# Experts' stage: VectorE forms a later group's variance inside the router's sequence of operations

## The reference

```python
h = layernorm(x) * (1 + ca) + sa
x = x + ga * attention(h)          # gated linear attention, 16 heads of 64
h = layernorm(x) * (1 + cb) + sb
# the experts' part: 8 experts, the best 2 count
p = softmax(max(h @ gate_W + gate_b, 1e-4))
comb = where(top2(p), max(p, 0.1) / sum over the two, 0)
y = einsum("bsd,edf->bsef", h, expert_W) + expert_b
x = x + gb * einsum("bsef,bse->bsf", y, comb) / 2
```

## Time and profile before

| | |
|---|---|
| median of 3 runs | 3374.94 us (3367.84 to 3376.30) |
| profiled execution | 3372.66 us |
| its span in the profile | 3370.9 us |
| mean granted TensorE clock | 0.991 of full speed |
| PE busy | 3237.4 us (96% of the span) |
| DVE busy | 2475.0 us (73%) |
| ACT busy | 1818.1 us (54%) |
| POOL busy | 1436.8 us (43%) |

### The profile page before, as it was taken

One profiled execution on the slowest core, in us unless ns is written; L12 is line 12 of the kernel. 1 busy time (PEld: TensorE's weight loads), 2 busy tenths in 40 slices (PEclk: granted clock), 3 DMA queues, 4 the chain that ended last, 5 costly groups with the idle time before them and its releaser, 6 DMA issues. The chain is left out here.

```text
span 3370.9 us, 129353 instructions
## 1 busy us (share of the span) xinstructions
PE 3237.4 (96%) x51114; PEld 2745.6 (81%) x51114; DVE 2475.0 (73%) x6681; ACT 1818.1 (54%) x4492; POOL 1436.8 (43%) x1117
## 2 busy tenths in 40 slices
PE   7999999999999999999999999999968999999999
PEld 6888888888888888888888888888856777777777
DVE  5777777776777777777777777777647878877886
ACT  5666666666666666666666666666633222222221
POOL 4444445545444444554554444455421222222222
PEclk9999999999999999999999999999988999999999
DMA  4222222222322222222223222222221111111110
GB/s 149 74 77 79 78 79 78 79 72 77 92 79 78 79 79 75 79 79 75 75 79 93 79 76 81 78 78 78 67 83 48 39 39 51 39 39 42 48 38 26
DMA packets 158613, 238.74 MB, mean 71 GB/s; under 512 B 30216, under 2 KB 82488, under 8 KB 157752
## 3 DMA queue, kind: packets, MB, share of 16 engines
q1 hardware_dynamic: 158008, 230.33, 21.6%
HBM read 194.58 MB, written 35.67 MB: 68 GB/s over the span
## 5 line engine op out<-in xcount | busy, mean ns | idle before, releaser
L447 POOL TENSOR_TENSOR qs_sb<-lam_bc,qk_sb 128x512 f32<-128x512 f32 x256 | 533.9, 2085 | 1080.7 <-DVE qk_sb L945 981.8
L554 ACT ACTIVATE kd_sb<-bank_scores,decay 128x64 f32<-128x64 f32 x2048 | 447.9, 330 | 287.7 <-PE bank_scores L820 279.0
L928 DVE SCALAR_TENSOR_TENSOR s_mid<-s_mid,lam_bc,bank_dense 128x65 f32<-128x65 f32 x1536 | 433.6, 282 | 55.1 <-DVE s_mid L928 0.3
L455 POOL TENSOR_TENSOR oT_lo<-oT,oT_hi 128x512 fp32r<-128x512 f32 x256 | 328.0, 1281 | 77.3 <-ACT oT_hi L531 77.0
L513 ACT ACTIVATE qk_sb<-bank 128x512 f32<-128x512 f32 x512 | 317.4, 620 | 50.7 <-PE bank L596 34.5
L515 ACT ACTIVATE qk_sb<-qk_sb 128x512 f32<-128x512 f32 x512 | 323.4, 632 | 16.3
L980 DVE TENSOR_TENSOR p_sb<-bank_scores,decay 128x512 f32<-128x512 f32 x256 | 176.5, 690 | 205.8 <-ACT kd_sb L554 203.8
L594 PE MATMUL bank<-wv_hi,h_hi 128*128 128x256 f32 x1024 | 307.4, 300 | 7.1 <-DVE qk_sb L943 3.3
L951 DVE TENSOR_TENSOR_SCAN decay<-a_bc,eye 128x512 f32<-128x512 f32 x256 | 311.0, 1215 | 2.0 <-DMA a_bc<-rows_dram 2.0
L1312 DVE SCALAR_TENSOR_TENSOR acc<-bank,comb,acc 128x256 f32<-128x256 f32 x512 | 230.1, 476 | 101.3 <-ACT acc L1180 91.8
L820 PE MATMUL bank_scores<-qk_sb 64*64 64x128 f32 x8192 | 287.4, 276 | 8.2 <-ACT oT_hi L531 4.3
(11 more groups left out here) (198 smaller groups left out, 8610.9 us busy)
## 6 DMA issues: line engine op xcount, KB each, us to landing
a_bc<-rows_dram SPq DMA_DIRECT2D x512, 128.0 KB, 3.0
lam_bc<-rows_dram SPq DMA_DIRECT2D x512, 128.0 KB
x_in<-in_L_attn_x_dram SPq DMA_DIRECT2D x32, 512.0 KB, 5.5
x_res<-in_L_attn_x_dram SPq DMA_DIRECT2D x32, 512.0 KB, 4.0
x_dram<-x_res SPq DMA_DIRECT2D x32, 512.0 KB, 2.9
x<-x_dram SPq DMA_DIRECT2D x32, 512.0 KB, 3.2
out_dram<-x SPq DMA_DIRECT2D x32, 512.0 KB, 2.9
ew_raw<-in_L_ffn_expert_W_dram SPq DMA_DIRECT2D x8, 256.0 KB, 5.4
```

What stands on the lines that cost most here:

```text
L447: pool.tensor_tensor(qs_sb[:, na, :], lam_bc[na][:, :], q_sb, ALU.mult).then_inc(qs_ready, 1)
L455: pool.tensor_tensor(oT_lo[:, u, :], oT32[:, :], oT_hi[:, u, :].bitcast(F32), ALU.subtract).then_inc(oT_lo_ready, 1)
L554: ins = act.activation(kd_sb[:, t, hd * DH:(hd + 1) * DH], KTR[:, hd, t * CK:(t + 1) * CK], ACT.Copy, scale=decay[:, hd, t, CK - 1:CK])
L928: dve.scalar_tensor_tensor(dst, src, lam_bc[nb][:, (ch + 1) * CK - 1:(ch + 1) * CK], U[ch], ALU.mult, ALU.add).then_inc(state_step, 1)
```

## The change

Inside groups that route the next group's tokens and have adds to do (T >= 0), the call ln_variance(T + 2) moves from behind route(T + 1) into it: between(k) issues it behind the add that follows operation 2 * NCH + 2 = 10 of twenty. NCH is 4. In group -1 it stays where it was (behind route), and in group -2 too (behind the four ln_stats). The number of instructions is the same on every engine; no DMA, no semaphore count and no other engine's order changes.

```diff
@@ -1415,17 +1415,21 @@
                             split_low(k // 2 - 1)
                     elif exists(T):
                         add(T, s, first + (k // 2 - 1 if k <= 2 * NCH else k - NCH - 1))
+                        if k == 2 * NCH + 2 and exists(T + 2):
+                            ln_variance(T + 2)
 
                 if exists(T + 1):
                     route(T + 1, (s + 1) % 2, between)
+                    if leads(T):
+                        ln_variance(T + 2)
                     adds(first + ROUTE - NCH, ADDS - BLOCK_ADDS)
                 else:
                     adds(first, ADDS - BLOCK_ADDS)
                     if exists(T + 2):
                         for ch in range(NCH):
                             ln_stats(T + 2, (s + 2) % GPB, ch)
-                if exists(T + 2):
-                    ln_variance(T + 2)
+                    if exists(T + 2):
+                        ln_variance(T + 2)
                 adds(ADDS - BLOCK_ADDS, ADDS)
                 if leads(T):
                     lo_rows = slice(2 * LO, EB_ROWS)
```

## The result

The changed kernel takes 3353.73 us (median of 6 runs, 3349.17 to 3360.70), beside 3375.62 us for the kernel before (6 runs, 3367.84 to 3377.47). The ratio is 0.994, with a 95% interval of 0.993 to 0.9949: some 20 us, or 0.6%, faster (17 to 24 by the interval). The forecast was 3351.2.

A forecast was written before the change was run, and what follows sets the result against it. TensorE, 96% busy, was taken to wait each group on the chain variance, shift, xn. 3372.66 - 23.8 + 0 = 3348.9 us, given as 3351.2 after a 2.3 us shift to the median; range 3346 to 3368.

The forecast's parts named there:

- Term 1: Experts' stage: TensorE's 29 waits for xn go, 16.8 us shown plus 0.24 us overlap each; gain 23.8 us.
- Term 2: Router on VectorE: the moved variance fills time L1368 stands held by GpSimd; cost 0, at most 0.60 us per group.
- Rival (a): Router's second half: GpSimd's power L1151 holds VectorE's L1372; TensorE waits 5.9 us in all, 3357.1 us; chance 0.25.
- Rival (b): Tenth place in the router: GpSimd's standing time doesn't cover the variance; costs 15.5 us, 3366.7 us; chance 0.14.
- (c): Router: L1368 misses the gap between L1140 and L1142, the power holds L1370; costs 35.3 us, 3386.5 us; chance 0.11.
- (d): Router: L1368 misses the gap between L1140 and L1142, the power doesn't block; costs 11.9 us, 3363.1 us; chance 0.05.
- (e): ScalarE: something else, its tile load or combT, keeps xn late, so no gain; 3375.0 us; chance 0.07.

The follow-up runs named there:

- k8: Variance behind the router's eighth operation instead of the changed kernel's tenth; 3373.82 us, ratio 1.0 to the kernel before.
- k14: Variance behind the router's fourteenth operation instead of the changed kernel's tenth, after GpSimd's large pair; 3367.77 us, ratio 0.9974 to the kernel before.
- k11: Variance behind the router's eleventh operation instead of the changed kernel's tenth, under GpSimd's second large operation; 3355.98 us, ratio 0.995 to the kernel before.
- k10_double_end: Changed kernel plus a second set of four bn_aggr into a spare tile declared last; 3358.84 us, ratio 0.9955 to the kernel before.
- k10_shift: Changed kernel plus an unused tile of 32 bytes per partition declared before var_eps, moving only addresses; 3362.11 us, ratio 0.9966 to the kernel before.
- k10_shift64: Changed kernel plus an unused tile of 64 bytes per partition declared before var_eps; 3351.21 us, ratio 0.9925 to the kernel before.

## Why the prediction was right

**What binds.** Shown: the chain from the variance to xn ended last, and with the variance early TensorE's wait went, in every version that moved it into the router, the slow k8 included.

**Term 1, 23.8 us.** Right in its size. The step from the idle time shown to what it is worth, 0.61 to 0.85 us by the earlier trace rows, was needed (the group of the earlier trace rows is the one at the turn of the loop, whose biases come late for that): the loop's groups became 0.84 us shorter (25.51 to 24.67) and the written-out ones 0.55 (25.22 to 24.67, for a wait shown as 0.32). With the shown 16.8 us alone the forecast would have been 5 us short. The reason given for the step, 0.24 us of overlap, was too simple: xn's first transposes start 0.47 us behind biases that last 0.64, an overlap of 0.17, and the other 0.06 us lie behind their start (6.55 us from the transposes to the gate matmuls before, 6.48 after). The groups gave 22.0 of 23.8. Part of the last 1.8 us lies in six groups (T = 0, 7, 12, 14, 19 and 26) in which L1252 comes 0.2 to 0.3 us late behind a late router, as it did in T = 12 before. In T = 7 and 19 VectorE stands 0.23 us before one of the router's adds, for nothing that the profile shows; the cause wasn't followed up.

**Not in the sum.** The 2.9 us by which the clock made the turn of the loop longer. They are about as much as the measured 3353.73 lies above the forecast, but single traces of one kernel differ by as much elsewhere, so this doesn't settle where the 2.5 us are.

**Term 2, 0 us.** Right, and for the reason given: k14 has the cost when the cover is missing (TensorE 0.47 us late, 0.54 expected), k11 shows that the second large operation covers as well, and k10_double_end shows the edge. One detail was wrong without harm: I had the tensor_scalar run free and L1368 asked for at once. It is held too. The time in which it is held L1368 would have been held too, so L1370 ends with L1142 as before; only the add behind L1368 starts 0.07 us later (2995.91, 7.84 us after the gate matmuls, for 7.77), which nothing waited for.

**Rival (a), the power.** Refuted: L1372 has two inputs in SBUF, was asked for 0.76 us into L1151 and took 0.18 us, and 0.17 or 0.18 in every other group. Asked for 0.18 us behind the power's start (L1373 behind L1152 in k10_double_end) or 0.26 us behind it (L1370 in k8) it isn't held either. The profile's spans on GpSimd are rough, but three places in one operation of 1.02 us leave little room for a hold. The Trainium skill's SBUF — State Buffer, section Who interferes with whom, has the second instruction block for the whole of the first. That agrees with L1140 and L1142, 1.3 us each, and doesn't with this short operation of 4 elements.

**Rival (b), no cover.** Its doubt was half right: var_eps, with one input, was held in the loop for 0.15 us. The Trainium skill's VectorE: DVE Perf Modes, section Mode 2×_2P, by which it reads through both ports, agrees with the trace here.

**Rivals (c) and (d), the missed gap.** The mechanism is real (k8, and the written-out groups of k10_double_end). The margin was read for the loop alone, as 0.19 us, and there it was wider: in k10_double_end var_eps was asked for 0.27 us later (7.76 us after the gate matmuls for 7.49), and L1368 still started 0.03 us before the second large operation, so it had been 0.3. The variance took 0.50 us up to L1368 where nothing held it, not 0.60. In the written-out groups it was narrower, 0.1 us: in the changed kernel L1368 starts 7.47 and L1142 7.58 us after the gate matmuls. By the prediction's own 0.60 us these six groups had only 0.05 to spare. That these got through is luck as much as reading. The price of (d) was too low as well: a group of k10_double_end that missed lost 0.54 us where it was written out, for 0.30, and 0.64 in the loop, for 0.42. I had counted only the router's end; the add behind L1368 also frees the bank for block 6, and k8 lost the whole gain by it where I had expected to keep half.

**(e)** didn't come about: xn started right behind combT.

## What to carry to other kernels

Look for instructions that take several times their usual length, and at what they end with. The standing time of one that is held by another engine is a free place for work that must be done early, if that work doesn't need what is held, or needs it no longer than the hold lasts. Find the edge too: here 0.3 us more put the next instruction behind a second hold in eight groups of thirty, and in most of these cost the whole gain (25.21 us a group, as before the change). And before giving an engine time back, see what its next instructions wait for; taking the holds away altogether bought nothing, because the adds behind them waited for products.

## What the runs showed of the hardware that was not expected

- A power of 4 elements per partition on GpSimd, 1.02 us long, doesn't hold a VectorE operation with two SBUF inputs (0.18 us when asked for 0.18, 0.26 or 0.76 us into it), though a 128x512 product does until it ends (L1370 in the changed kernel stands to 0.05 us behind the end of L1142).
- VectorE's float32 tensor_scalar of 4 elements per partition is held like one with two inputs (1.31 us in k8 for 0.17), bn_aggr is not (0.37 us for four beside L1140, 0.38 without it).
- 32 bytes in the start address of h and the tiles with it change the pitch of the experts' 128x512 matmuls from 0.229 to 0.233 us, 24.67 to 25.02 us per group. With 64 bytes they are 0.228 and 24.64. The granted clock was 1.00 from 2700 to 2950 us in k10_shift and in k10_shift64. Which of the moved tiles does it wasn't tried.
- A TensorE wait shown as 0.61 us costs 0.84, and one shown as 0.32 costs 0.55; 0.17 us of the difference are the overlap of the transposes with the biases before them, which a wait takes away.
- After TensorE had stood for 3.1 us, its granted clock stayed 1.00 in the kernel before and was 0.50 for the next 5.2 us in the changed one, with 0.43 us per matmul for 0.23. What decides between the two isn't shown.
